# Low parts of the projection weights on GpSimd, and the first values earlier in the first scores of a cross-attention block

## The reference, cut to what matters

```python
xq  = layer_norm(x, qn_w, qn_b);  ctx = layer_norm(context, cn_w, cn_b)
q   = (xq @ q_w).reshape(B, N, H, D)
kv  = (ctx @ kv_w).reshape(B, M, 2, H, D);  k, v = kv[:, :, 0], kv[:, :, 1]
attn = einsum('bnhd,bmhd->bhnm', q, k) * D ** -0.5
attn = where(mask, -finfo.max, attn);  attn = softmax(attn)
out = einsum('bhnm,bmhd->bnhd', attn, v).reshape(B, N, C) @ proj_w + proj_b
x   = x + out
h   = layer_norm(x, n2_w, n2_b)
return x + gelu(h @ fc1_w + fc1_b) @ fc2_w + fc2_b
```

## Time and profile before

| | |
|---|---|
| median of three runs | 1045.58 us |
| profiled execution: its own time | 1045.75 us |
| profiled execution: span | 1044.0 us |
| TensorE matmul busy | 1029.6 us (99%) |
| VectorE busy | 822.4 us (79%) |
| ScalarE busy | 434.4 us (42%) |
| GpSimd busy | 358.7 us (34%) |
| mean granted TensorE clock | 0.998 |

### The profile page before, as it was taken

How to read it: one execution, slowest core, us unless ns; L and a number is a source line. 1 busy time by engine, 2 the same in 40 slices (tenths; PEclk the granted TensorE clock), 3 DMA queues, 4 the chain that set the end, 5 groups by cost and what they waited for, 6 DMA issues and landing times.

```text
span 1044.0 us, 15433 instructions
## 1 busy us (share of the span) xinstructions
PE 1029.6 (99%) x5857; PEld 855.9 (82%) x5857; DVE 822.4 (79%) x1323; ACT 434.4 (42%) x766; POOL 358.7 (34%) x259
## 2 busy tenths in 40 slices
PE   8999999999999999999999999999999999999998
PEld 6788888888888777888878888888888888888887
DVE  7899999999997898887887677686766677666655
ACT  5344344444454565445543333353434352232221
POOL 3466566667788663233404000304000300300000
PEclk9999999999999999999999999999999999999999
DMA  7012122212210186554466635346436343734312
GB/s 268 9 46 71 54 88 75 63 62 85 80 43 22 67 306 227 197 209 184 181 225 249 241 132 191 113 168 235 172 131 240 112 181 124 301 123 170 128 64 80
DMA packets 52790, 149.22 MB, mean 143 GB/s; under 512 B 11313, under 2 KB 19545, under 8 KB 44531
## 3 DMA queue, kind: packets, MB, share of 16 engines
q1 hardware_dynamic: 52139, 147.25, 39.5%
q10 hardware_dynamic: 584, 1.06, 0.3%
HBM read 108.13 MB, written 39.85 MB: 142 GB/s over the span
## 4 chain that ended last, share of the span: by engine, by line
PE 94%; DVE 4%; DMA 0%; issue 0%; ACT 0%; POOL 0%; SPq 0%; DVEq 0%; ACTq 0%
PE bank L1801 33%; PE bank L1771 28%; PE bank L1604 8%; PE bank L1648 8%; PE bank L1585 5%; PE bank L1636 4%; PE bank L1617 3%; PE bank L1780 1%; PE bank L1595 1%; PE bank L1567 1%; PE bank L1625 1%; DVE w1r L1366 1%; DVE acc L1409 1%; DVE gT L1401 0%; DMA rows<-in_L_xattn_cn_w 0%; DVE hop L1371 0%
## 5 line engine op out<-in xcount | busy, mean ns | idle before, releaser
L1801 PE MATMUL bank<-w2r,gT 128*128 128x512 f32 x1536 | 359.7, 391 | 2.1 <-DVE acc L1409 2.0
L1801 PEld LDWEIGHTS bank<-w2r,gT 128*128 128x128 f32 x1536 | 286.6, 188 | 64.1 <-DVE acc L1409 5.1
L1771 PE MATMUL bank<-hop,w1r 128*128 128x512 f32 x1344 | 312.4, 390 | 1.7 <-DVE hop L1371 0.7
L1771 PEld LDWEIGHTS bank<-hop,w1r 128*128 128x128 f32 x1344 | 251.2, 188 | 55.2 <-issue 2.2
L1409 DVE TENSOR_TENSOR acc<-bank,acc 128x512 f32<-128x512 f32 x256 | 176.6, 691 | 104.5 <-PE bank L1801 98.1
L1396 DVE TENSOR_TENSOR ybuf<-bank,ybuf 128x512 f32<-128x512 f32 x224 | 148.6, 688 | 81.2 <-PE bank L1771 73.1
L1046 ACT ACTIVATE ybuf<-ybuf,cols 128x512 f32<-128x512 f32 x128 | 91.6, 716 | 153.4 <-DVE ybuf L1396 153.4
L684 POOL TENSOR_TENSOR S<-S,rsum 128x1232 f32<-128x1232 f32 x32 | 75.3, 2354 | 61.6 <-DVE rsum L1202 61.6
L649 POOL TENSOR_TENSOR hrs<-hve,mhalf 128x1 f32<-128x1 f32 x32 | 18.0, 564 | 218.5 <-DVE hve L1381 218.5
L1401 DVE TENSOR_TENSOR gT<-ybuf,gT 128x512 fp32r<-128x512 f32 x128 | 93.1, 748 | 0.0
L792 POOL TENSOR_TENSOR acc<-acc,fc2b 128x512 f32<-128x512 f32 x32 | 43.4, 1371 | 125.4 <-DMA acc<-x_scratch 125.1
(11 more groups left out here) (111 smaller groups left out, 1448.3 us busy)
## 6 DMA issues: line engine op xcount, KB each, us to landing
w1r<-w_scratch SPq DMA_DIRECT2D x24, 1792.0 KB, 7.3
w2r<-w_scratch SPq DMA_DIRECT2D x24, 1024.0 KB, 4.9
w_scratch<-w1r SPq DMA_DIRECT2D x8, 1792.0 KB, 6.3
xr<-in_x SPq DMA_DIRECT2D x32, 256.0 KB, 3.0
x_scratch<-xr SPq DMA_DIRECT2D x32, 256.0 KB, 2.0
hring<-x_scratch SPq DMA_DIRECT2D x32, 256.0 KB, 3.0
acc<-x_scratch SPq DMA_DIRECT2D x32, 256.0 KB, 3.9
w_scratch<-w2r SPq DMA_DIRECT2D x8, 1024.0 KB, 4.9
```

Source lines behind the costliest of these rows:

```text
L1771: mm = pe.matmul(bank_[:, :], w1r[:, w1_slot(s), c, w, kk * P:(kk + 1) * P], hop[i][:, d, kk, :], start=(kk == 0 and n == 0), stop=(kk == ...
L1801: mm = pe.matmul(bY[t % 2][:, :], gT[s % 2][:, j, d, t * P:(t + 1) * P], w2r[:, s % 2, j, w, :], start=(n == 0), stop=(n == 5))
```

## The change

It has three parts. VectorE no longer makes the low parts of the projection weights; GpSimd does, at the end of its step "q", and TensorE waits for GpSimd's semaphore in place of VectorE's. On VectorE the statistics of unit 2 come ahead of `q_lo(0)`. On TensorE `values(0)` moves from behind `score(0, 3)` to behind `score(0, 1)`, ahead of `x_T(1)`.

```diff
@@ GpSimd, step, prep == "q"
                 negative(k.plus(2))
                 x_rstd()
+                for c in range(KT):
+                    pool.wait_ge(a_wp, c + 1)
+                    pool.tensor_tensor(wp[LO][:, c, :], praw[:, c, :], f32(wp[HI][:, c, :]), ALU.subtract).then_inc(p_wp, 1)
                 return
@@ VectorE
-        def proj_weights(tiles):
-            for k in tiles:
-                dve.wait_ge(a_wp, k + 1)
-                dve.tensor_tensor(wp[LO][:, k, :], praw[:, k, :], f32(wp[HI][:, k, :]), ALU.subtract).then_inc(v_wp, 1)
@@ VectorE, step, prep == "q"
                 keys_lo(1)
                 q_bias()
-                proj_weights(range(KT))
-                q_lo(0)
                 n = k.plus(4)
                 stats()
+                q_lo(0)
                 v_bn.wait(dve, n, UT - 1)
                 variance()
                 q_lo(1)
@@ TensorE, step, prep == "scores"
                 score(0, 0)
                 score(0, 1)
+                values(0)
                 x_T(1)
                 score(0, 2)
                 score(0, 3)
-                values(0)
                 for g_ in range(KT):
                     score(1, g_)
                 for m in range(KT):
                     q(m)
                 values(1)
-                pe.wait_ge(v_wp, KT)
+                pe.wait_ge(p_wp, KT)
```

More of the change, by code:

```diff
@@ L254, in build_block @@
     t_keys, a_keys, v_keys, t_vals, a_vals = (sem(n) for n in ("t_keys", "a_keys", "v_keys", "t_vals", "a_vals"))
-    t_qbias, v_qbias, v_wscale, a_wq, v_wq, a_wp, v_wp = (sem(n) for n in ("t_qbias", "v_qbias", "v_wscale", "a_wq",
-                                                                           "v_wq", "a_wp", "v_wp"))
+    t_qbias, v_qbias, v_wscale, a_wq, v_wq, a_wp, p_wp = (sem(n) for n in ("t_qbias", "v_qbias", "v_wscale", "a_wq",
+                                                                           "v_wq", "a_wp", "p_wp"))
     a_ctxT = sem("a_ctxT")
```

## The result

The changed kernel takes 1047.47 us (median of 13 runs, 1046.67 to 1048.19) against 1045.58 us (13 runs, 1044.13 to 1046.38) for the kernel before. The ratio is 1.0016 with a 95% interval of 1.0009 to 1.0023: slower by 1.7 us, between 0.9 and 2.4. The forecast was 1047.2 us, a loss of 1.63. The profiled execution took 1047.47 us with a span of 1045.7.

The account below looks back on a forecast made before the run. TensorE, busy 1029.6 of 1044.0 us, and a chain over the other engines were taken to tie at step 0's start. 3.43 for `values(0)` less 1.80 of halts adds 1.63 to 1045.75: 1047.38, as median 1047.2, range 1045.3 to 1048.4.

Parts of the forecast that it names:

- The two halts: TensorE's waits for `q_lo` ahead of `x_T(0)` (0.65 us) and `x_T(1)` (1.15) would go, winning 1.80.
- `values(0)` in front of the last scores of tile 0: On TensorE its 3.43 us, less 1.80 won, would complete tile 0's scores and start `maximum(0)` 1.63 later.
- The gain given back at `q(0)`: TensorE would wait 1.78 us for `x_lo` ahead of `q(0)`, giving back the 1.80 won.
- The second chain without slack: From tile 0's scores through VectorE, GpSimd and ScalarE to step 0's first score: all 1.63 us later.
- The tie at the start of step 0: TensorE's own work and the chain over the other engines both end at 46.1, at most 0.1 us apart.
- GpSimd's cover: GpSimd's four subtractions, 1.305 us each, would end near 27.3, before anything waits for GpSimd: cost 0.
- The upper bound of 2.51 each: Longest time taken for each GpSimd subtraction, the doubled figure for a busy partner; the four would end at 32.2.
- the upper bound of 0.25: Most that GpSimd's subtractions would slow VectorE, in us, from 22.1 to 27.3; 0 was taken.
- A: Rival: TensorE's gaps alone count, so 1.80 us faster (1043.8), or unchanged at 1045.6; chance 0.12 for both forms.
- B: Rival: TensorE's longer halts ahead of `q(0)` and step 0 lower its clock, costing 2 us more: 1049.2; chance 0.09.
- C: Rival: GpSimd holds every VectorE instruction between 22.1 and 27.3, so all ends 4.4 us later: 1051.6; chance 0.04.

Follow-up runs that it names:

- e1: Changed kernel with `values(0)` put back behind `score(0, 3)`, so only the low parts on GpSimd and the earlier statistics remain: 1044.47 us.
- e2: Kernel before with only `values(0)` moved ahead of `x_T(1)`, low parts left on VectorE: 1047.82 us.
- e5: Changed kernel with VectorE's two `normed` instructions moved to between and behind the masked tiles: 1045.82 us.
- e6: Kernel before with VectorE's two `normed` instructions moved to between and behind the masked tiles: 1045.29 us.
- e3: e1 with one of the four matmuls of `values(0)` ahead of `x_T(1)` and three behind `score(0, 3)`: 1045.03 us.
- e8: Changed kernel with eight more GpSimd subtractions of the same shape, into unused spare tiles, ahead of the four: 1052.01 us (4 runs).
- e4: e3 with VectorE's two `normed` instructions moved to between and behind the masked tiles: 1043.43 us.
- e7: e1 with VectorE's two `normed` instructions moved to between and behind the masked tiles: 1044.58 us.

## Why the prediction was right

**The two halts.** Right: 0.65 and 1.15 forecast as won, and neither wait is in the profile after. `x_T(0)` starts 5.99 behind the reference instruction (27.55 - 21.56), forecast was 5.98 (27.26 - 21.28). e1 prices the first part alone at 1.0, as was forecast for it.

**`values(0)` in front of the last scores of tile 0.** Right, and it is the cause: `maximum(0)` was forecast 1.63 later, and it is 12.71 behind the reference instruction (34.27 - 21.56) against 11.11 (32.39 - 21.28), 1.60 later. e2 shows it by itself.

**The gain given back at `q(0)`.** Right: a halt of 1.78 was forecast, the profile gives 1.55 idle time (TensorE's ends are modelled and hide about 0.2), and `q(0)` starts 15.40 behind the reference instruction against 15.54.

**The second chain without slack.** Right, and shown by e5 and e6: where the chain is made shorter, the changed kernel gains 1.5 and the kernel before 0.2. The tie at the start of step 0, read as 45.96 + 0.14 = 46.10, was the reading on which the sign hung. Its margin was put too small: the prediction has at most 0.1 us between the two chains, e6 shows 0.2, with TensorE's as the earlier one. That changes nothing in the sum, which follows the later chain.

**GpSimd's cover.** Right: 5.03 us for the four, 1.26 each against an estimate of 1.305, the end at 27.49, and no effect on TensorE's start. The upper bound of 2.51 each is the duration of no row of this shape (1.305 doubled is 2.61), and nothing hangs on it. The one VectorE instruction that was held, `veps`, took 0.52 where it took 0.17 before. These 0.35 are more than the upper bound of 0.25 that the prediction gave, and in e3 the same instruction took 1.03. It did no harm because VectorE waits behind it for ScalarE's high part (still 1.10 us here, 0.58 in e3). e8 bounds the cover: twelve are too many. The Trainium skill, GPSIMD Engine Reference, section 1 (Specifications), names VectorE instructions in a 2-port mode or with two SBUF inputs as those that contend with GpSimd. The rows agree as far as they go: `normed` and `veps` were held (1.50 for 0.54, 0.52 for 0.17), `stats` (1.29 for two against 1.27) and `q_lo` (0.86 against 0.87) were not. No row tells in which mode `normed` and `veps` ran.

**The rivals.** A fell with e2 (slower where it said 1.2 faster) and e5. B's mechanism is real, but not at the halts of 1.55 and 1.56 that this change makes: the granted clock of the changed kernel, in the figure behind the busy times, stays at 1.00 over both halts:

```profile
36.00:38.00 2.00, 1.04 (x8) 1.04 (x9) 2.00 (x3) 0.00 (x0) 2.00 (x1) 1.00 0.00 0
...
47.00:48.00 1.00, 0.03 (x1) 0.03 (x1) 0.83 (x3) 0.04 (x1) 0.79 (x1) 1.00 0.10 15
48.00:50.00 2.00, 2.00 (x16) 2.00 (x17) 0.91 (x2) 0.36 (x1) 2.00 (x2) 1.00 0.04 6
```

This reading needs a second witness, for at the start of the program the same profile reads 1.00 from 8 to 10 us, where a group of twelve 128-column matmuls took 2.93 us; in the kernel before the group took 2.66, with 0.52 read there. The spacing of the matmuls gives it. From the first to the fourth matmul of step 0 it is 0.53 us before and after (46.10 to 46.63, 47.97 to 48.50), and 0.93 in e8 (50.24 to 51.17), where the clock reads 0.50; and the stretch from `q(0)` to `values(1)` behind the first halt takes 5.86 us (36.96 to 42.82) against 5.76, the 0.1 lying in its first matmul (36.96 to 37.18).

C fell with e1.

**What stays open.** The median moved by 1.89 and the trace by 1.59; the interval of the runs (0.9 to 2.4) holds both, and nothing here tells whether the 0.3 is more than scatter. That the forecast median came within 0.3 of the measured one is partly luck; the forecast of 1.63 against 1.59 by the trace is not, since its steps agree one by one.

## What to carry to other kernels

An idle gap of the busiest engine is not free space: work put there moves all that stands behind it in that queue, and if what stands there starts a chain over other engines to the next stage, the gap comes back further on. Before filling one, add up the chain from the displaced instruction to the next point where the queues meet, and compare its end with the filler's engine; fill with a piece no longer than the gap, and only when the second chain has slack (e3 against e4). When two chains tie, shortening either one alone gives next to nothing (e3 and e7 against e4).

## What the runs showed of the hardware

- A VectorE `tensor_scalar` on SBUF that meets a running GpSimd `tensor_tensor` is held until about the end of that instruction, whatever its own size: 1.50 in place of 0.54 for 128x512, 0.52 to 1.03 in place of 0.17 for 128x2. In the seven kernels with the subtractions on GpSimd the 128x2 one ends 0.02 to 0.04 us behind the fourth of them, wherever it began. The next one in GpSimd's queue does not extend the hold (e8).
- In the profiled executions a halt of TensorE of 1.9 us (e5) left the granted clock at 1.00, and one of 4.39 us (e8) was followed by some 3 us of work at 0.50, which cost 1.3 us.
- Before the change can act, the profiled executions already differ: the reference instruction starts at 20.34 in e3 and at 21.81 in e1. The medians of 11 to 13 runs still agree with the traces to some 0.6 us once each trace is measured from an event inside it, while single spans do not (e3's of 1041.9 us looks like a gain of 2.1 and is one of 1.0). What sets this start was not tried.
